# Mamba block with a SwiGLU FFN on one core: a second buffer of states, the multiplication by C one scan later, residual sums by TensorE, a plain fp32 FFN, and the first batch's products in another order

## The reference, cut to what matters

```python
# x: (8 batches, 512 steps, 128); d_inner 256, 16 states, 4 taps, dt rank 64, hidden 384
h = x * rsqrt(mean(x * x) + 1e-5) * norm_w
xs, res = split(h @ in_proj_w.T)
u = silu(causal_conv(xs, conv_w) + conv_b)
delta, Bm, Cm = split(u @ x_proj_w.T, [64, 80])
delta = softplus(delta @ dt_proj_w.T + dt_proj_b)
state = exp(delta * A) * state + delta * u * Bm      # over the 512 steps, 256 x 16 of them
y = sum_n(state * Cm) + u * D
y = (y * silu(res)) @ out_proj_w.T + x
x1 = layernorm(x + y)
hid = silu(x1 @ wg.T) * (x1 @ wu.T)                   # int weights times 1/127
out = layernorm(x1 + hid @ wd.T)
```

## Time and profile before

| what | value |
|---|---|
| time, median of 3 runs | 610.42 us (609.94 to 611.24) |
| the profiled execution, its own time | 610.23 us |
| its span (first to last instruction) | 608.5 us |
| TensorE clock granted, mean | 0.838 of full |
| DVE busy | 534.5 us |
| POOL busy | 398.3 us |
| ACT busy | 355.9 us |
| share of the chain that ended last: DVE, issue, POOL, PE, ACT | 37%, 22%, 16%, 10%, 7% |
| DVE idle ahead of scans, until POOL's product | 9.9 us in 8 waits |
| DVE idle ahead of scans, until ACT's decay | 16.7 us in 14 waits |

### The profile page before, as it was taken

One profiled execution on the slowest core, in us unless ns is written; L12 is line 12 of the kernel. 1 busy time (PEld: TensorE's weight loads), 2 busy tenths in 40 slices (PEclk: granted clock), 3 DMA queues, 4 the chain that ended last, 5 costly groups with the idle time before them and its releaser, 6 DMA issues.

```text
span 608.5 us, 5732 instructions
## 1 busy us (share of the span) xinstructions
PE 425.8 (70%) x1477; PEld 172.9 (28%) x1477; DVE 534.5 (88%) x582; ACT 355.9 (58%) x594; POOL 398.3 (65%) x176
## 2 busy tenths in 40 slices
PE   4898586786598595887598695887597694467353
PEld 3332121322232241323232241322242241113142
DVE  4779997989998998989998999989998999999822
ACT  2675874496547675496547775497537774443221
POOL 5588597567776777576776688566776688575000
PEclk9988886997988987987988787987988787777756
DMA  8084044300660044400560043400660044400000
...
DMA packets 27360, 39.11 MB, mean 64 GB/s; under 512 B 3816, under 2 KB 10056, under 8 KB 27344
## 3 DMA queue, kind: packets, MB, share of 16 engines
...
...
## 4 chain that ended last, share of the span: by engine, by line
DVE 37%; issue 22%; POOL 16%; PE 10%; ACT 7%; SPq 4%; DMA 3%; DVEq 1%; POOLq 0%; ACTq 0%
DVE state L904 19%; POOL prod L742 11%; DVE weighted L913 9%; SPq L326 4%; DMA du_rep<-z_wm 2%; PE dense_ps L449 2%; DVE g L920 1%; POOL rs L762 1%; ACT decay_ps L554 1%; DVE g_act L955 1%; PE dense_ps L447 1%; PE y_ps L427 1%; ACT L578 1%; ACT x L565 1%; DVE g_act L951 1%
## 5 line engine op out<-in xcount | busy, mean ns | idle before, releaser
L904 DVE TENSOR_TENSOR_SCAN state<-decay_ps,prod 128x512 f32<-128x512 f32 x256 | 299.2, 1208 | 32.1 <-ACT decay_ps L554 16.7
L742 POOL TENSOR_TENSOR prod<-du_rep,b_rep 128x2048 f32<-128x2048 f32 x63 | 284.8, 4530 | 41.5 <-DVE state L904 35.7
L554 ACT ACTIVATE decay_ps<-delta_rep,a_neg 128x512 f32<-128x512 f32 x252 | 169.8, 687 | 74.6 <-DVE state L904 74.2
L913 DVE TENSOR_TENSOR weighted<-state,c_ps 128x2048 f32<-128x2048 f32 x64 | 146.4, 2287 | 2.7 <-DVE state L904 0.6
L416 PE MATMUL c_ps<-xd,pick 96*128 96x512 f32 x128 | 84.4, 747 | 86.3 <-DVE weighted L913 86.3
L427 PE MATMUL y_ps<-weighted,gather 128*32 128x512 f32 x512 | 87.2, 760 | 6.4 <-DVE weighted L913 6.4
L762 POOL TENSOR_TENSOR rs<-ve,powm 128x4 f32<-128x4 f32 x16 | 16.2, 1012 | 104.5 <-ACT nm L560 104.5
L447 PE MATMUL dense_ps<-h_t,tap_t 128*128 128x512 f32 x128 | 58.9, 604 | 6.5 <-ACT h_t L599 6.5
L416 PEld LDWEIGHTS c_ps<-xd,pick 96*128 96x128 f32 x128 | 25.0, 222 | 120.0 <-DVE weighted L913 111.9
L559 ACT ACTIVATE ve<-mv 128x4 f32<-128x4 f32 x16 | 3.3, 206 | 71.4 <-DVE mv L939 44.1
L746 POOL TENSOR_TENSOR z_wm<-z_e,z_wm 128x512 f32<-128x512 f32 x15 | 18.7, 1269 | 30.3 <-ACT z_wm L622 25.3
...
## 6 DMA issues: line engine op xcount, KB each, us to landing
...
```

The source lines that it names most:

```text
L554: A(decay_ps[n % DECAYS][:, :], decay_ps[n % DECAYS][:, :] if spread_first else delta_rep[:, h, c, :], ACT.Exp, scale=a_neg[:, col:col + 1 ...
L742: TT(prod[quad % 2][:, :, :], du_rep[:, h, :, :], b, ALU.mult).then_inc(prod_ready, 1)
L904: dve.tensor_tensor_scan(state[:, n % BLOCKS, :], decay_ps[n % DECAYS][:, :], prod[n // BLOCKS % 2][:, n % BLOCKS, :], 0.0, ALU.mult, ALU. ...
L913: TT(weighted[quad % 2][:, :, :], state[:, :, :], c_ps[:, :].unsqueeze(1).broadcast_to([P, BLOCKS, T]), ALU.mult).then_inc(weighted_ready, 1)
```

## The change

`state` becomes a pair of buffers, one for even and one for odd quads, and a scan waits for a `weigh` only once per quad, for that of two quads before. `weigh` of a quad moves behind the first scan of the next quad; that of quad 7 stands behind scan 0 of the next batch. TensorE adds 2x to the projection (4 matmuls with `twice`, the identity times 2) and x1 to the down projection (4 with the identity); ACT copies r1 from PSUM at step 7, and the second layer norm reads the one bank of `down`. The FFN's gate and up matmuls take x1 in fp32 (one matmul each) instead of two fp32r matmuls of x1_hi and x1_lo. Most steps of `dense` move by one. In batch 0, POOL makes the products of quads 0 to 2 before `soften` and `scale_u` of the second half, and ACT's `late_copies` come after exp 2.

```diff
-        state = sb("state", [P, BLOCKS, T])
+        state = pair("state", [P, BLOCKS, T])
...
-                ["C", "S", "down0", "down1", "b2", "b3"],
+                ["C", "S", "down", "b2", "b3"],
...
-                "down0": 0, "down1": 1, "b2": 2, "b3": 0}
+                "down": 0, "b2": 1, "b3": 2}
...
                     for i in range(TILES):
                         for h in range(HALVES):
-                            last = mm(ps[:, i * P:(i + 1) * P], g[:, h, i * P:(i + 1) * P],
-                                      out_t[:, h, :], start=(h == 0), stop=(h == HALVES - 1))
+                            mm(ps[:, i * P:(i + 1) * P], g[:, h, i * P:(i + 1) * P], out_t[:, h, :],
+                               start=(h == 0), stop=False)
...
+                        last = mm(ps[:, i * P:(i + 1) * P], twice[:, :], xk, start=False, stop=True)
...
                     if name == "gate0":
-                        it.wait(pe, x1_hi_ready, 1, -1, 1)
                         it.wait_taken(pe, "x1")
-                    w = (gate_t if kind == "gate" else up_t)[:, n, :]
-                    mm(ps[:, :], w, x1_hi[:, :], start=True, stop=False)
-                    last = mm(ps[:, :], w, x1_lo[:, :], start=False, stop=True)
+                    last = mm(ps[:, :], (gate_t if kind == "gate" else up_t)[:, n, :], x1_t[:, :], start=True, stop=True)
                 elif kind == "down":
                     it.wait_taken(pe, f"up{HID - 1}")
-                    for i in range(2):
+                    for i in range(TILES):
                         for b in range(HID):
-                            last = mm(ps[:, i * P:(i + 1) * P], g_act[:, b, (2 * n + i) * P:(2 * n + i + 1) * P],
-                                      down_t[:, b, :], start=(b == 0), stop=(b == HID - 1))
+                            mm(ps[:, i * P:(i + 1) * P], g_act[:, b, i * P:(i + 1) * P], down_t[:, b, :],
+                               start=(b == 0), stop=False)
+                        last = mm(ps[:, i * P:(i + 1) * P], ident[:, :], x1[:, i, :], start=False, stop=True)
...
-                    if step == 10:
+                    if step == 11:
                         it.wait(act, g_ready, HALVES, -1, HALVES)
                         for name, dst in (("xs", u), ("res", sres)):
...
-                    if step == 22:
+                    if step == 23:
                         it.wait(act, z_step, 4, 1, 3)
                         A(z_ln[:, :, :], z_e[:, :, :], ACT.Ln, bias=1.0).then_inc(ln_ready, 1)
-                    for q, at in enumerate((23, 24, 27, 28)):
+                    for q, at in enumerate((24, 25, 27, 28)):
...
-                    if step == 8:
+                    if step == 7:
+                        it.wait_full(act, "proj")
+                        it.take(A(r1[:, :, :], it.ps("proj")[:, :].rearrange("p (i m) -> p i m", m=M), ACT.Copy), "proj")
+                    if step == 10:
                         shift_scale(it, mv1, mv1_ready, ve1, nm1, ve1_ready)
...
-                    for b, at in enumerate((18, 19, 21)):
+                    for b, at in enumerate((19, 20, 21)):
...
-                    if it.k0 == 0 and n == 0:
+                    if it.k0 == 0 and n == 1:
                         late_copies()
...
                 if it.k0 == -1:
                     late_setup()
                     error(it, 1)
-                    soften(it, 1)
-                    scale_u(it, 1)
                     it.wait_taken(pool, "b0")
...
                         multiply(it, quad)
-                    if it.outs and quad == 2:
+                        if it.k0 == 0 and quad == 2:
+                            soften(Iteration(-1), 1)
+                            scale_u(Iteration(-1), 1)
+                    if it.outs and quad == 3:
...
-                it.wait(dve, weighted_ready, QUADS, 0, n // BLOCKS)
+                if n % BLOCKS == 0:
+                    it.wait(dve, weighted_ready, QUADS, 0, n // BLOCKS - 1)
...
                     if step == 27:
-                        for n in range(2):
-                            it.wait_taken(dve, f"down{n}")
+                        it.wait_full(dve, "down")
                         for i in range(TILES):
-                            last = dve.bn_stats(st2[:, i, :], r2[:, i, :])
+                            last = dve.bn_stats(st2[:, i, :], it.ps("down")[:, i * P:(i + 1) * P])
...
                 for n in range(GROUPS):
-                    if it.outs and n in (7, 28):
-
-                        it.wait(dve, ln1_step if n == 7 else ln2_step, 1, -1, 1)
                     if it.scan:
                         scan(it, n)
-                        if n % BLOCKS == BLOCKS - 1:
-                            weigh(it, n // BLOCKS)
+                    if it.outs and n in (8, 28):
+                        it.wait(dve, ln1_step if n == 8 else ln2_step, 1, -1, 1)
+                    if it.scan:
+                        if n % BLOCKS == 0 and n > 0:
+                            weigh(it, n // BLOCKS - 1)
+                        elif n == 0 and it.outs:
+                            weigh(it, QUADS - 1, -1)
                     dense(it, n)
+                if it.k0 == B - 1:
+                    weigh(it, QUADS - 1)
```

More of the change, by code:

```diff
@@ L335, in iteration @@
                 if it.outs:
-                    done, row = value(it.count(1, -1, 1)), value((it.k0 - 1 + it.ahead) * T)
+                    done, row = value(it.job_count("down")[1]), value((it.k0 - 1 + it.ahead) * T)
                 if it.ins:
@@ L357, in iteration @@
                     rows = y_rows[row:row + T, :] if isinstance(row, int) else y_rows[bass.ds(row, T), :]
-                    sp.wait_ge(y_ready, done)
+                    sp.wait_ge(taken[BANK["down"]], done)
                     sp.dma_start(rows.rearrange("(i t) m -> t i m", t=P), y_out[it.next][:, :, :]
@@ L516, in iteration @@
                                 spread_c(it, quad)
-                            if it.k0 == 0 and quad == 0:
-                                spread_delta(DECAYS)
                         elif name == "S":
@@ L645, in dense @@
                         act.wait_ge(y_free[it.next], 16 + 16 * ((it.k0 - 1) // 2) + 8 * it.ahead)
-                        normalise(it, y_out[it.next], r2, rs2, nmr2, shift2_ready, y_ready)
+                        ps = it.ps("down")
+                        it.take(normalise(it, y_out[it.next], lambda i: ps[:, i * P:(i + 1) * P], rs2, nmr2,
+                                          shift2_ready), "down")
             def head(it):
@@ L940, in dense @@
                         last.then_inc(mv1_ready, 1)
-                    if step == 16:
-                        it.wait(dve, x1_hi_ready, 1, -1, 1)
-                        it.take(TT(x1_lo[:, :], it.ps("x1")[:, :], x1_hi[:, :].bitcast(f32), ALU.subtract), "x1")
-                if it.scan and step == 18:
+                if it.scan and step == 19:
                     combine(it, 0, 0)
                 if it.outs:
-                    for b, (at, then) in enumerate(((19, 20), (20, 21), (22, 23))):
+                    for b, (at, then) in enumerate(((20, 21), (21, 22), (23, 24))):
                         if step == then:
```

77 lines of the change are left out of this document (33 added, 44 removed).

## The result

The changed kernel takes 644.42 us (median; 640.34 to 646.52 in 4 runs), beside 610.18 for the kernel before: ratio 1.055, 95% interval 1.0489 to 1.061, so 5.5% slower. 645 had been said. The profiled execution took 646.52, with a span of 644.7, and is the longest of the four.

The account below looks back on a forecast made before the run. A chain from softplus's Ln through copies and POOL's product to the next scan 0 was taken as the bound. 608.5 + 23.1 (six batches) + 5.3 (batch 0) + 2.9 (batch 7) + 3.3 (tail) = 643.1 span, forecast 645, range 627 to 659.

Parts of the forecast that it names:

- The price of W7 behind s0: Scan 0 to W4: quad 7's multiplication now stands behind the next batch's scan 0, +2.20 us a batch.
- scan 4's decay behind h_t: Scan 0 to W4: ACT issues exp 4 only behind h_t, so scan 4 starts late, +2.33 us a batch.
- The three stretches: A batch: s0 to W4 41.4 us, W4 to the Ln's end 10.9, from there to s0' 19.95; sum 72.2, +3.85.
- s0 of batch 1: End of batch 0: product 4 comes late and holds scan 16, so this scan starts at 105.6, +5.3 us.
- DVE's waits for itself: Scan 0 to W4: waits between DVE's own scans, W and statistics removed, -1.40 us a batch.
- rival 4: DVE's scans and W keep the old pitch, its waits for itself return nothing: 653 us, chance 0.03.
- The FFN: Gate 2 in fp32 at TensorE's low clock level +0.8 us, x1_lo removed -0.58 a batch; tail +1.1.
- 19.95 us that no engine's load sets: Ln's end to s0': 2.74 `soften`, 4.13 SP's issues, 8.53 issues and landing, 4.55 product; unchanged.
- Rival 2: DVE is the bound and gets shorter if copies land before s0' is wanted: about 578 us, chance 0.08.
- The tail: After batch 7: more matmul records in proj and down, FFN in fp32, less x1_lo and r2: +3.3 us (2.5 to 4).
- rival 1: Only the order of W7 costs, exp 4 and gate 2 don't come late: 628 us, chance 0.12.
- Rivals 2 and 3: DVE is the bound and gets shorter, about 578 us, chance 0.08; the edits cancel, 610 us, chance 0.03.

Follow-up runs that it names:

- w7_ahead: Changed kernel with only the multiplication by C of quad 7 back ahead of the next batch's scan 0: 618.52 us, ratio 1.013.
- pool_order_back: Changed kernel with only POOL's order in the head and batch 0 as before the change: 641.07 us, ratio 1.0527.
- pair_only: Kernel before with a pair of state buffers only, each W still behind its fourth scan: 604.72 us, ratio 0.9894.
- du_first: Changed kernel with only SP's order altered, delta * u of the first half copied ahead of delta in every batch: 638.44 us, ratio 1.0454.
- ln_step22: Changed kernel with only softplus's Ln back at step 22, ahead of exp 24: 668.09 us, ratio 1.0949.
- w_moved_only: Kernel before with two state buffers and every W behind the next quad's first scan, all else as before: 674.51 us, ratio 1.1048.

## Why the prediction was right

**The price of W7 behind s0** was the main term: +2.20, and +2.33 for scan 4's decay behind h_t. w7_ahead gives back 25.9 us, 4.1 a batch. That is 0.45 less than their sum: 0.56 returns as scan 4's wait for product 1. The second term is what scan 4 measured: g waits 0.7 and scan 4 1.25 to 1.7, 1.9 to 2.4 in all.

**The three stretches** came out within 0.12 each in the batch shown (41.28 for 41.4, 10.90 for 10.9, 19.90 for 19.95). Over the six batches they are 41.3 to 43.7, 9.95 to 10.9 and 19.5 to 20.6, with means of 42.0, 10.6 and 20.0, so the forecast was 0.6 short in the first and 0.3 long in the second. Single steps came out too: s0 of batch 1 at 105.59 for 105.6, W4 of batch 0 at 79.42 for 79.1, and its product 4, at 65.58 for 66.1, waiting for a DMA and holding scan 16:

```profile
65.58 8.99 POOL L744 TENSOR_TENSOR prod<-du_rep,b_rep 128x2048 f32<-128x2048 f32 x2 [8.08 <-DMA du_rep<-z_wm]
```

```profile
70.22 1.22 DVE L910 TENSOR_TENSOR_SCAN state<-decay_ps,prod 128x512 f32<-128x512 f32 x1 [4.29 <-POOL prod L744]
```

In batch 0 scan 28 also waits, 2.76 us for product 7, which it didn't before. The prediction hadn't seen that, and s0 of batch 1 still came where it was said. It isn't the move of POOL alone: in pool_order_back the same scan waits 2.59 for its decay.

**DVE's waits for itself** returned what the pitches said: scan to W 251.47 - 250.33 = 1.14 (1.26 before), W to scan 253.65 - 251.47 = 2.18 (2.29 + 0.21 = 2.50 before). By the rule of the Trainium skill (VectorE: DVE Perf Modes, The DRAIN you can't avoid) nothing would have come of it. pair_only takes away only the wait of a scan for the W ahead, and is 1.1% faster, so rival 4 and the rule are out for this kernel. The same section of the Trainium skill adds that a next instruction which isn't held starts earlier. The trace agrees: the scan at 253.65 starts 0.08 ahead of the end of W, at 251.47 + 2.26 = 253.73.

**The FFN** cost about what it was priced at: gate 2 +0.8 in six batches and 1.1 in the tail, less x1_lo's 0.58 in six batches, is 2.4; measured 3.0 (613.19 against 610.14). In the profiles of those two runs the six batches give 1.0, the tail 1.1, and batch 7 another 1.05, which had no term. The low level of gate 2 was a choice between two values, and in the change it came in four of the six batches.

**Where the working was off.** Four places:

1. "19.95 us that no engine's load sets" made the copies the end of the batch, and the layer norm's chain a tie. In the kernel before, product 0 starts 0.26 to 0.28 behind the layer norm's numbers in four of the six batches ("issue" and not the DMA in the earlier trace rows), so the 19.95 was there the length to the end of the layer norm's chain, and the copies' own is at most that. In the change the copies are last by 0 to 1.5 and the distance is 20.0 in the mean, so the number held, in part by luck. But du_first and ln_step22 show that the loop from the aggregate to s0', 6.9 us, is what can't be left. Rival 2's condition, the Ln 3.4 us sooner, wouldn't have freed DVE: with the copies out of the way it waits 3.18 all the same.
2. The six batches took 25.2 and not 23.1. Most of it is the one batch at 74.63, where the projection ran at the low level and DVE waited 1.8 for r1. That the projection could do so was in no term; only res and down had such bounds. The profiled execution is also 2.1 above the median. The four times span 6.2 us, so that 645 meets the median to within 0.6 is partly luck.
3. DVE's busy time fell by 22.4, not by about 17. A W takes 2261 ns in the middle now, not 2287, which is 1.7 of it. It didn't touch the time.
4. The tail (the rest in the table) cost 2.45, not 3.3, just under its lower bound of 2.5.

**The rivals.** The order of W7 is the largest cost, but without it the change is still 1.3% slower, so rival 1 as a whole (628) isn't what happened: scan 4 did wait for its decay in all six batches, and gate 2 came late in four. Rivals 2 and 3 fell with the waits before s0'.

**What stays open:** how the 30 us between w_moved_only and the change divide over its other edits, and why TensorE's level at the projection differs between batches of one execution.

## What to carry to other kernels

A change that frees a buffer and one that uses the freedom to reorder are two changes, and should be timed apart: here the first gave 1.1%, the reordering and the other edits lost 6.6% on it, and the reordering alone 11.5%. Before moving work off the end of a loop, measure the loop that it was hiding (from the aggregate to the next scan, 6.9 us, 3.7 of them covered without W7 and 6.0 with it), since work that stands in such a gap is free and work that leaves it is not. Then look for work to put into the gap: W6 behind the aggregate took the last 0.9 us away, and a wait further on showed itself at once.

## What the runs showed of the chip beyond that

- The same eight matmul records of the projection took 3.70 us at a granted clock of 1.00 and 5.8 at 0.62, in one kernel and one execution. Where it was 5.8, DVE waited up to 3.6 us a few instructions on.
- A semaphore wait between two neighbouring instructions of DVE cost 0.12 us (scan to W) and 0.3 (W to scan), although both run on the same engine in order (1.26 against 1.14 and 2.50 against 2.18 start to start, before and in the change).
- An Ln one decay sooner, 0.7 us of ACT's time, cost 24 us (3.7%): scan 24's decay stood behind it, and with that scan the W, the down projection and the next batch.
